# One program in place of two in a gated delta-rule layer: setup joined to the heads, gate logits summed by shifted weights, x's norm on ScalarE, the last norms cut in pieces

## The chip, the cores and the metric

The kernel runs on one core of one Trainium2 chip. The metric is the device time of one execution in microseconds (us); lower is better. The engines of the core are named as in the profile: PE (TensorE; PEld is its weight load), DVE (VectorE), ACT (ScalarE), POOL (GpSimd) and SP (SyncE), which here only issues DMAs. Each engine runs its own instructions in order, and waits on semaphores for the others.

## What is computed

The input x is 8 sequences of 512 tokens with 256 features. `_layernorm` has no weights.

```python
x = x + _layernorm(_L0_attn_ref(_layernorm(x), Wqkv, Wz, Wb, Wa, conv_w, A_log, dt_bias, norm_w, Wout))
x = x + _layernorm(_L0_ffn_ref(_layernorm(x), W1, b1, W2, b2, W3, b3))

# _L0_attn_ref: 16 heads, q, k and v of 128 features each
qkv = silu(causal_conv_4_taps(x @ Wqkv));  z = x @ Wz
beta = sigmoid(x @ Wb)                                  # one logit for a head and a token
g = -exp(A_log) * softplus(x @ Wa + dt_bias)            # another one
q, k = l2norm(q) * 128**-0.5, l2norm(k)
for each token:                                         # M is 128 x 128 for a head
    M = M * exp(g);  M = M + k (v - k M) * beta;  o = q M
out = (o * rsqrt(mean(o*o) + 1e-6) * norm_w * silu(z)) @ Wout
# _L0_ffn_ref: 256 -> 512 -> 512 -> 256, with relu after the first two layers
```

## The kernel before, in words

**Two programs.** `gated_delta_mlp` runs `normalise_and_gate` (the setup) and then `delta_heads`. Between them all semaphores of the first are cleared and all engines meet (L69).

**Setup.** Eight sequences b go through a loop. DVE: `statistics(b + 1)` (L186 to L192), `normalise(b)` (L197: four operations of 128x256), `low_parts(b - 1)` (L204). POOL takes the root of the variance (L173, a `pow` on 128x4). PE transposes the normed x (L293) and multiplies it by the gate weights (L304: six matmuls of 512 columns). ACT copies the transposed x as its rounded high part (L266) and the 32x512 logits (L271). Each product in this kernel that needs full precision is three matmuls: high by high, high by low, low by high. SP stores the logits and the two parts of x^T in DRAM (L148, L152). Then the logits of all sequences are read back from DRAM with one (head, sequence) pair on each of the 128 partitions (L156, L157), and DVE and ACT make of them beta, the decays and their cumulated products (L228 to L258), a chain of 128x512 operations in which each waits for the one before. The decays go to DRAM as rows (L159, L160).

**Heads.** `delta_heads` loads its weights and constants, splits the first head's weights into high and low (`split`, POOL, L603 and L605) and runs 128 pairs (16 heads by 8 sequences) in a software pipeline written out by hand: in iteration a of `range(PAIRS + LAST_STAGE)` each engine does the projections and the convolution of pair a (`project` L1254, `convolve` L790 and L966, `activate` L802), the block inverse of pairs a-1 and a-2, the state recurrence of pair a-3 (`solve` L1361, `state` L1062, `from_state_k` L1368) and the output of pair a-4 (`gated` L1096, `out_project` L1402, `take_sum` L872, `add` L680). The order on each engine is the order of these calls. `decays(a)` (DVE, L977) needs a row of decays loaded from DRAM.

**Drain.** Iterations a = 128 to 131 have no projection any more. Their `fill` calls put in the start of the feed-forward part, sequence b = a - 128: DVE `fill(0)` is `attn_statistics(b)`, `fill(1)` is `add_input(b)` (norm of the attention's sum L1121, addition of x L1136, statistics of the second norm L1109 to L1116), `fill(2)` is `normed_input(b)` (L1121 into `xn`). POOL `root` (L713) takes the two roots; POOL's `split_second` (L690, L692) and `split_third` (L700, L702) split the weights of layers 2 and 3 in quarters: a cast and a subtraction for each. In DVE's order `state(2, a - 3)` and `residual(a - 2)` stand behind `fill(1)`, and the next iteration stands behind `fill(2)`.

**Feed-forward loop.** For b = 1 to 7, PE does `second_layer(b, 0..2)`, `turn_input(b + 1)` (L1419, eight transposes of `xn`), `second_layer(b, 3)`, `first_layer(b + 1, 0..3)`, `third_layer(b)` (all L1425). All turned tiles and all hidden tiles take turns in two PSUM banks, g0 and g1. ACT does `turned_high` (L882) and `hidden` (L897, L900), POOL `hidden_low` (L708) and `root`, and DVE in its iteration b: `result(b)` (L1160 and statistics of four chunks), `finish(b)` (norm L1121 and addition L1168), `turned_low(b + 2)` (L1149), `normed_input(b + 3)`, `attn_statistics(b + 4)`, `add_input(b + 4)`.

## Time and profile before

| | us |
|---|---|
| median of the 3 timed runs (2787.2 to 2790.44) | 2787.56 |
| the profiled execution, its own time | 2786.65 |
| its span, first to last instruction | 2784.90 |
| setup: start to the first convolution step on DVE | 107.02 |
| gate math: its first to its last operation | 65.58 to 87.76 |
| iterations a = 128 to 131 and the first third layer, about | 2485 to 2592 |
| feed-forward loop and end | 2597 to 2785 |

The page gives the busy time of each engine over the whole span; the windows view gives it by stage; the timeline shows the order on each engine, with the idle time before an instruction and what ended it in square brackets. The granted clock of PE is a share: 1.00 is 2.4 GHz, 0.50 is 1.2 GHz, and a value between is a mean of stretches at either.

### The profile page before, as it was taken

How to read it: one execution, taken by the hardware profiler on the slowest of the kernel's cores; microseconds unless marked ns; L12 is line 12 of the kernel's file. 1: busy time of each engine (PE TensorE's matmuls, PEld its weight loads, DVE VectorE, ACT ScalarE, POOL GpSimd, SP SyncE). 2: the span in 40 equal slices, each digit the busy share in tenths (PEclk: the TensorE clock that was granted, in tenths of full speed). 3: DMA queues.
4: the chain of work that ended last, by engine and by line, in shares of the span. 5: the costliest groups of instructions: out<-in, count | busy, mean ns of one | idle time of the engine just before them, and what ended most of it. 6: DMA issues, size and time to landing. Idle time of an engine off the chain costs nothing.

```text
span 2784.9 us, 70958 instructions
## 1 busy us (share of the span) xinstructions
PE 2636.6 (95%) x23924; PEld 2308.0 (83%) x23924; DVE 2305.1 (83%) x4996; ACT 2189.9 (79%) x7350; POOL 2023.3 (73%) x1802
## 2 busy tenths in 40 slices
PE   3399999999999999999999999999999999997898
PEld 2288888888888888888888888888888888885776
DVE  5588888888888888888888888888888888885683
ACT  2388888888888888888888888888888888873343
POOL 2267777877777787777777877777787777775553
PEclk9799999999999999999999999999999999997999
DMA  5322222222222222222222222222222223210110
GB/s 197 112 80 102 92 88 83 102 92 72 99 94 91 81 100 94 79 90 101 89 82 92 102 75 88 100 92 79 94 100 80 91 92 125 71 58 23 31 39 23
DMA packets 81011, 241.94 MB, mean 87 GB/s; under 512 B 8720, under 2 KB 23952, under 8 KB 64272
## 3 DMA queue, kind: packets, MB, share of 16 engines
q1 hardware_dynamic: 80656, 237.41, 24.4%
q8 instruction: 198, 3.24, 0.5%
q14 instruction: 157, 1.29, 0.2%
HBM read 223.75 MB, written 13.63 MB: 85 GB/s over the span
## 4 chain that ended last, share of the span: by engine, by line
PE 86%; DVE 4%; issue 2%; POOL 2%; ACT 1%; DMA 0%; SPq 0%; DVEq 0%; POOLq 0%; ACTq 0%
PE pj L1254 25%; PE pj L1402 9%; PE tr L1261 9%; PE g L1301 8%; PE st L1361 5%; PE op L1381 4%; PE op L1382 4%; PE st L1391 4%; PE st L1368 3%; PE bk L1320 2%; PE bk L1331 2%; PE bk L1334 2%; PE g L1425 2%; PE bk L1351 1%; PE g L1320 1%
## 5 line engine op out<-in xcount | busy, mean ns | idle before, releaser
L966 DVE SCALAR_TENSOR_TENSOR conv<-pj,cw,conv 128x511 f32<-128x511 f32 (+2 forms) x1152 | 847.5, 745 | 54.6 <-ACT conv L790 40.6
L1254 PE MATMUL pj<-xt,w_hi 128*128 128x512 f32 x2048 | 684.3, 415 | 17.3 <-ACT y L779 17.3
L644 POOL TENSOR_TENSOR kq<-kq,cum 128x512 f32<-128x512 f32 x256 | 442.0, 1747 | 0.0
L1254 PE MATMUL pj<-xt,w_lo 128*128 128x512 f32 x1024 | 404.0, 395 | 0.0
L1254 PEld LDWEIGHTS pj<-xt,w_hi 128*128 128x128 f32 x2048 | 348.4, 190 | 63.8 <-ACT y L779 17.7
L673 POOL TENSOR_TENSOR inv<-inv,x 128x512 f32<-128x512 f32 x128 | 148.3, 1159 | 340.0 <-ACT inv L849 340.0
L790 ACT ACTIVATE conv<-pj,cw 128x512 f32<-128x512 f32 x384 | 266.4, 694 | 123.3 <-PE pj L1254 113.3
L1043 DVE TENSOR_TENSOR y<-bk,mask 128x256 f16<-128x256 f32 x512 | 216.5, 423 | 163.7 <-PE bk L1320 157.3
L680 POOL TENSOR_TENSOR attn<-attn,part 128x512 f32<-128x512 f32 x256 | 326.6, 1276 | 0.0
L809 ACT ACTIVATE squares_out<-tr 128x128 bf16<-128x128 f32 x1024 | 273.7, 300 | 46.0 <-PE tr L1261 46.0
L1402 PE MATMUL pj<-wo,yt 128*128 128x256 f32 x1024 | 285.5, 401 | 0.8 <-DVE yt L1096 0.8
L841 ACT ACTIVATE x<-bk 128x256 f16<-128x256 f32 x512 | 196.5, 384 | 111.9 <-PE bk L1334 100.9
L611 POOL TENSOR_TENSOR b<-b,f 128x512 f32<-128x512 f32 x128 | 149.4, 1167 | 142.8 <-DVE f L1005 142.8
L1301 PE MATMUL g<-kq 128*128 128x256 f32 x1024 | 242.3, 379 | 0.0
L809 ACT ACTIVATION_READ_ACCUMULATOR squares_out<-tr 128x1 f32 x1024 | 235.2, 231 | 0.0
L1254 PEld LDWEIGHTS pj<-xt,w_lo 128*128 128x128 f32 x1024 | 193.0, 188 | 45.2
L784 ACT ACTIVATE u<-st,f 128x128 f32<-128x128 f32 x512 | 195.7, 382 | 42.9 <-PE st L1361 20.5
L872 ACT ACTIVATE part<-pj,oc 128x256 f32<-128x256 f32 x512 | 215.5, 477 | 16.3 <-POOL oc L667 6.6
L1361 PE MATMUL st<-r,inv 128*128 128x128 f32 x1024 | 216.5, 293 | 3.2 <-DVE r L1078 1.6
L1361 PEld LDWEIGHTS st<-r,inv 128*128 128x128 f32 x1024 | 164.3, 190 | 57.1 <-DVE r L1078 23.9
L1301 PEld LDWEIGHTS g<-kq 128*128 128x128 f32 x1024 | 184.8, 190 | 19.8
L1382 PE MATMUL op<-u,qk 128*128 128x128 f32 x1024 | 198.7, 276 | 0.0
(201 smaller groups left out, 7877.8 us busy)
## 6 DMA issues: line engine op xcount, KB each, us to landing
xt<-xt_scratch SPq DMA_DIRECT2D x128, 1024.0 KB, 4.8
decay<-decay_scratch SPq DMA_DIRECT2D x128, 256.0 KB, 5.3
cum<-cumdecay_scratch SPq DMA_DIRECT2D x128, 256.0 KB, 5.6
w_raw<-in_w_heads SPq DMA_DIRECT2D x16, 512.0 KB, 7.0
xt_scratch<-xt_hi SPq DMA_DIRECT2D x8, 512.0 KB, 2.8
xt_scratch<-xt_lo SPq DMA_DIRECT2D x8, 512.0 KB, 3.8
x_in<-in_x SPq DMA_DIRECT2D x8, 512.0 KB, 4.2
out<-kq SPq DMA_DIRECT2D x16, 256.0 KB, 2.3
```

Of the source, the lines that this page charges most:

```text
L644: last = nc.gpsimd.tensor_tensor(part, part, of(cum, p)[:, :], ALU.mult)
L680: nc.gpsimd.tensor_tensor(rows, rows, part[:, 2 * i:2 * i + 2, :], ALU.add).then_inc(added[i], 1)
L790: nc.scalar.activation(conv[:, i, :], pj[:, i % 2, :], ACT.Copy, scale=cw[:, i, p // NSEQ, TAPS - 1:TAPS]).then_inc(pre[i], 1)
L809: last = nc.scalar.activation(squares_out[:, row, c, :], tr[:, c, :], ACT.Square, accum_out=of(sums, p)[:, row, c:c + 1])
L966: nc.vector.scalar_tensor_tensor(out=conv[:, i, j:SEQ], in0=pj[:, i % 2, 0:SEQ - j], scalar=cw[:, i, p // NSEQ, TAPS - 1 - j:TAPS - j], in ...
L1043: nc.vector.tensor_tensor(y[level][:, :, :].rearrange("p c (g two w) -> p c g two w", two=2, w=w)[:, :, :, 0, :], ps[:, 0:CH * HALF].rearr ...
L1254: last = nc.tensor.matmul(pj[:, i % 2, :], w[:, kt, cols], x_[:, kt, :], start=(n == 0), stop=(n == 3 * KT - 1))
L1261: last = nc.tensor.transpose(tr[:, c, :], src(c), ident[:, :])
L1301: last = nc.tensor.matmul((g0, g1)[c // 2][:, cols], of(kq, p)[:, 0, chunk(c)], of(kq, p)[:, :, chunk(c)], start=True, stop=True)
L1361: nc.tensor.matmul(st[:, 1, :], of(inv, p)[:, c, :], r[:, c, :], start=True, stop=True).then_inc(w_done[c], 1)
L1382: mm = nc.tensor.matmul(op[:, c, :], of(qk, p)[:, c, :], u[:, c, :], start=(c == 0), stop=True)
L1402: last = nc.tensor.matmul(pj[:, i, DM * (c % 2):DM * (c % 2) + DM], yt[:, chunk(c)], of(wo, p // NSEQ)[:, :], start=True, stop=True)
```

## The change

**Start.** `normalise_and_gate` is gone; `delta_heads` does the setup at its head, with no barrier, on its own buffers: x^T of the eight sequences goes through six places that overlie buffers of the heads, and the last two sequences in the loop (order 2..7, 0, 1) stay in `xt[0]` and `xt[1]`, where pairs 0 and 1 find them. x comes in eight loads. The loop is now, on DVE, `statistics_of_x(i + 1)`, `low_x(i)`; on POOL `root_of_x(i)` (the `pow`, then a multiplication that gives the shift), with one `split` of the first head's weights after each of roots 1 to 4; on ACT `normed(i + 1)` (four 128x256 activations with a bias and a scale from memory) and then `high_x(i)`; on PE `turn_x(i + 1)`, `gate_logits(i)`.

**Gates.** The gate weights stand in a zero-padded tile, 8 columns apart. A window of 128 columns that is shifted by the sequence's number puts a head's logit on partition 8 h + b and zeros elsewhere, so that all sequences add up in two PSUM banks (beta's and the decay's): 12 matmuls a sequence. The way through DRAM (L148, L156, L157) is gone. Of the gate math, the `max` moves under an activation, the memset of `tc` to POOL, the last reciprocal behind the scan. `take_beta` and `decays(0)` move to the end of DVE's iteration 0. ACT's constants (`y`, `ident16`) come before its last gate exponential, and the `memset` of `attn` goes behind the setup.

**Semaphores.** Groups of semaphores for the chunks (`tap`, `w_done`, `u_ready`, `km_done`, `mu_done`, `m_ready`, `w_copied`) become one each that is counted on, in the order in which they were signalled before.

**Drain and feed-forward loop.** The norms on DVE come in ten pieces of two chunks each, spread over the iteration, with the last two (`xn`) at the head of the next. The high parts of the weights of layers 2 and 3 are cast by ACT (`high_weights`, two of 128x512 in each of iterations 128 to 130, ahead of `take_sum(0)`), and POOL subtracts in two operations of 128x512. From b = 2 on the turned x goes to the banks `tr` and `bk`, and `turn_input(b + 1)` stands ahead of `second_layer(b, 2)`; `turned_high` moves likewise. `result` and `finish` work by halves.

```diff
-            statistics(0)
-            for b in range(NSEQ):
-                if b + 1 < NSEQ:
-                    statistics(b + 1)
-                normalise(b)
-                if b:
-                    low_parts(b - 1)
-            low_parts(NSEQ - 1)
+            statistics_of_x(0)
+            for i in range(NSEQ):
+                if i + 1 < NSEQ:
+                    statistics_of_x(i + 1)
+                low_x(i)
+            gate_decays()
...
+            def normed(i):
+                act.wait_ge(rstd_done, 2 * i + 2)
+                for c in range(CH):
+                    last = nc.scalar.activation(of(xin, i)[:, c, :], of(xin, i)[:, c, :], ACT.Identity,
+                                                bias=shift[:, i % 3, c:c + 1], scale=rs[:, i % 3, c:c + 1])
+                last.then_inc(x_normed, 1)
+
+            def high_x(i):
+                if i >= 6:
+                    act.wait_ge(xt_out[i - 6], 2 * DMA)
+                for kt in range(KT):
+                    act.wait_ge(turned_x, KT * i + kt + 1)
+                    nc.scalar.activation(xt_at[i][0][:, kt, :], turn_bank[(KT * i + kt) % 4], ACT.Copy).then_inc(hi_done, 1)
+
+            normed(0)
+            for i in range(NSEQ):
+                if i + 1 < NSEQ:
+                    normed(i + 1)
+                high_x(i)
...
+            def root_of_x(i):
+
+                pool.wait_ge(s_var_done, i + 1)
+                nc.gpsimd.tensor_tensor(rs[:, i % 3, :], ve[:, i % 3, :], halves[:, 1, :], ALU.pow).then_inc(rstd_done, 1)
+                pool.wait_ge(rstd_done, 2 * i + 1)
+                nc.gpsimd.tensor_tensor(shift[:, i % 3, :], shift[:, i % 3, :], rs[:, i % 3, :], ALU.mult).then_inc(rstd_done, 1)
+
+            pad_gate_weights()
+            for i in range(NSEQ):
+                root_of_x(i)
+                if 1 <= i < 5:
+                    split(i - 1, 0)
...
+            def gate_logits(i):
+
+                window = slice(GAP - FIRST[i], GAP - FIRST[i] + P)
+                hi, lo = xt_at[i]
+                for kt in range(KT):
+                    pe.wait_ge(hi_done, KT * i + kt + 1)
+                    for gate_ in range(2):
+                        for w in (wg_hi, wg_lo):
+                            nc.tensor.matmul(logit_bank[gate_], w[kt][:, gate_, window], hi[:, kt, :],
+                                             start=(i == 0 and kt == 0 and w is wg_hi), stop=False)
...
             for a in range(PAIRS + LAST_STAGE):
                 convolve(V, 3, a - 1)
+                fill(8, a)
                 mask_level(3, a - 2)
                 inverse_norm(a - 1)
+                fill(9, a)
                 decay_b(a - 1)
...
                 mask_level(5, a - 2)
-                decays(a)
+                if a:
+                    decays(a)
+                fill(0, a)
                 mask_level(1, a - 1)
...
                 convolve(Q, 1, a)
-                fill(0, a)
+                fill(1, a)
                 convolve(Q, 2, a)
                 mask_level(2, a - 1)
                 convolve(Q, 3, a)
+                fill(2, a)
                 convolve(K, 1, a)
-                fill(1, a)
+                fill(3, a)
                 convolve(K, 2, a)
+                fill(4, a)
                 state(2, a - 3)
                 convolve(K, 3, a)
+                fill(5, a)
                 residual(a - 2)
                 rhs(3, a - 3)
                 convolve(V, 1, a)
-                fill(2, a)
+                fill(6, a)
                 convolve(V, 2, a)
+                fill(7, a)
                 norms(a)
+                if a == 0:
+                    take_beta()
+                    decays(a)
...
+    def turned_tile(b, kt):
+
+        return sums_of(place["turn", b, kt]) if b < 2 else (flat(tr), bk[:, :])[kt]
...
             for b in range(1, NSEQ):
-                for n in range(HT - 1):
+                for n in range(HT):
+                    if n == HT - 2 and b + 1 < NSEQ:
+                        turn_input(b + 1)
                     second_layer(b, n)
-                if b + 1 < NSEQ:
-                    turn_input(b + 1)
-                second_layer(b, HT - 1)
```

## Rows read from the trace of the kernel before

**Rows 1.** The page, part 1: busy time of each engine.
```profile
PE 2636.6 (95%) x23924; PEld 2308.0 (83%) x23924; DVE 2305.1 (83%) x4996; ACT 2189.9 (79%) x7350; POOL 2023.3 (73%) x1802
```
**Rows 2.** Windows, 400 us of pairs: stretch, length, busy us, granted clock, DMA.
```profile
600.00:1000.00 400.00, 399.85 (x3802) 352.47 (x3801) 349.30 (x749) 346.16 (x1197) 315.16 (x280) 1.00 0.25 91
```
**Rows 3.** Timeline, one pass of the setup loop: start, length, instruction, idle before.
```profile
35.49 1.39 DVE L186 BATCH_NORM_STATS2 stats<-xin 128x6 f32<-128x256 f32 x4
...
37.28 1.37 DVE L197 TENSOR_SCALAR xin<-xin,mv,rstd 128x256 f32<-128x256 f32 x4
...
37.45 1.24 POOL L173 TENSOR_TENSOR rstd<-rstd,minus_half_s 128x4 f32<-128x4 f32 x1 [3.03 <-DVE rstd L192]
37.83 1.05 ACT L266 ACTIVATE xt_hi<-s_ps 128x512 fp32r<-128x512 f32 x2
...
38.58 1.28 DVE L204 TENSOR_TENSOR xt_lo<-s_ps,xt_hi 128x512 fp32r<-128x512 f32 x2
...
39.77 1.39 DVE L186 BATCH_NORM_STATS2 stats<-xin 128x6 f32<-128x256 f32 x4
```
**Rows 4.** Lines view, whole span: forms that stand nearest to the new operations.
```profile
L872 ACT ACTIVATE part<-pj,oc 128x256 f32<-128x256 f32 x512 | 215.5, 477 | 16.3 <-POOL oc L667 6.6 <-issue 1.6 <-PE pj L1402 0.9
...
L841 ACT ACTIVATE x<-bk 128x256 f16<-128x256 f32 x512 | 196.5, 384 | 111.9 <-PE bk L1334 100.9
...
L680 POOL TENSOR_TENSOR attn<-attn,part 128x512 f32<-128x512 f32 x256 | 326.6, 1276 | 0.0
...
L702 POOL TENSOR_TENSOR w_lo<-w_raw,w_hi 128x256 fp32r<-128x256 f32 x4 | 2.9, 733 | 0.3
```
**Rows 5.** Timeline of ACT in the drain: four activations of `take_sum` in a row.
```profile
2550.98 1.57 ACT L872 ACTIVATE part<-pj,oc 128x256 f32<-128x256 f32 x4 [2.38 <-POOL oc L667]
```
**Rows 6.** DMA view, first 18 us: KB each, us from issue to landing.
```profile
xin<-in_x SPq DMA_DIRECT2D x1, 512.0 KB, 4.1
```
**Rows 7.** Timeline of the gate math.
```profile
65.58 0.49 DVE L228 TENSOR_SCALAR al<-al,dtb 128x512 f32<-128x512 f32 x1 [8.89 <-DMA al<-logits_scratch]
...
79.59 0.43 DVE L243 TENSOR_SCALAR al<-al 128x512 f32<-128x512 f32 x1
...
80.97 0.72 ACT L279 ACTIVATE tb<-td,rate 128x512 f32<-128x512 f32 x1 [13.05 <-DVE rate L246]
81.43 3.35 DVE L249 RECIPROCAL bl<-bl 128x512 f32<-128x512 f32 x1
...
85.81 1.22 DVE L256 TENSOR_TENSOR_SCAN td<-tb,tc 128x512 f32<-128x512 f32 x1
```
**Rows 8.** Timeline, the first convolution steps on DVE.
```profile
107.02 4.54 DVE L966 SCALAR_TENSOR_TENSOR conv<-pj,cw,conv 128x511 f32<-128x511 f32 x6 [3.77 <-ACT conv L790]
```
**Rows 9.** Timeline of PE in the drain: its long waits.
```profile
2508.20 0.80 PE L1368 MATMUL st<-m,kq 128*128 128x128 f32 x2 [5.02 <-DVE m L1062]
...
2536.03 0.80 PE L1368 MATMUL st<-m,kq 128*128 128x128 f32 x2 [5.16 <-DVE m L1062]
...
2567.11 0.56 PE L1368 MATMUL st<-m,kq 128*128 128x128 f32 x2 [4.34 <-DVE m L1062]
...
2596.83 0.76 PE L1425 MATMUL g<-h_hi,xt 128*128 128x512 f32 x1 [4.70 <-POOL last_h L708]
```
**Rows 10.** Timeline of DVE in iteration 128.
```profile
2504.61 1.23 DVE L1136 TENSOR_TENSOR attn<-attn,x_in 128x1024 f32<-128x1024 f32 x1
...
2512.30 2.96 DVE L1121 TENSOR_SCALAR xn<-attn,mmv,rs 128x256 f32<-128x256 f32 x4 [2.85 <-POOL rs L713]
```
**Rows 11.** PE's waits from 2600 us to the end: us in total, times, longest.
```profile
PE g L1425 <- DVE x_lo L1149: 8.0, 6, 1.4
```
**Rows 12.** Timeline, one pass of the feed-forward loop.
```profile
2634.51 1.28 DVE L1149 TENSOR_TENSOR x_lo<-g,x_hi 128x512 fp32r<-128x512 f32 x2
2635.25 0.50 PE L1425 MATMUL g<-h_hi,xt 128*128 128x512 f32 x1 [1.39 <-DVE x_lo L1149]
```
**Rows 13.** Windows, one such pass: PE, PEld, DVE, ACT, POOL, granted clock, DMA.
```profile
2630.40:2657.10 26.70, 24.97 (x129) 21.00 (x129) 20.59 (x46) 11.54 (x19) 14.01 (x12) 0.94 0.13 40
```

More of the change, by code:

```diff
@@ L961, in _, with take_beta @@
+            def take_beta():
+                dve.wait_ge(beta_turned, 1)
+                then(nc.vector.tensor_copy(beta[:, :, :], logit_bank[1].rearrange("p (c n) -> p c n", c=CH)))
+            statistics_of_x(0)
+            for i in range(NSEQ):
+                if i + 1 < NSEQ:
+                    statistics_of_x(i + 1)
+                low_x(i)
+            gate_decays()
             dve.wait_ge(consts_in, 7 * DMA)
```

694 lines of the change are left out of this document (340 added, 354 removed).

## The prediction, made before the changed kernel ran

> **What bounds the kernel now.** I read the busy times first: PE 2636.6 of 2784.9 us [rows 1]. The windows then say where that is a bound: between 600 and 1000 us PE is busy for 399.85 of 400 us at the full clock [rows 2]. The 128 pairs are PE's, and nothing there can gain unless PE's own work shrinks; the change leaves that work alone. What is left are the two ends, where PE waits. The setup holds the first convolution step on DVE back until 107.02 us [rows 8]. In the drain PE waits three times for a state from DVE, 5.02, 5.16 and 4.34 us, and once 4.70 us for POOL [rows 9]. In the feed-forward loop it waits six times for `x_lo`, 8.0 us in all [rows 11], and a pass of 26.70 us has PE busy for 24.97 us at a mean clock of 0.94 [rows 13].
>
> **Setup loop: no gain, rather a loss.** Before, a pass takes 39.77 - 35.49 = 4.28 us [rows 3], paced by DVE, which holds statistics, `normalise` (1.37) and `low_parts`; roots and ACT work go on beside it. In the new order each step waits for the one before, across engines: DVE does statistics(i+1) only after low(i-1); POOL's root(i+1) needs them; ACT has `normed(i+1)` ahead of `high_x(i)`; low(i) needs `high_x(i)`. One pass is therefore the sum of the chain. Statistics to the start of the root: 37.45 - 35.49 = 1.96, and 0.08 for the added shift operation. Root 1.24. Second POOL operation, 128x4, plus two handovers: the trace has no such multiplication. Its bounds are 0.1 and 1.24 (the `pow` itself); a POOL operation with two inputs takes 733 ns on 256 columns and 1276 on 512 [rows 4], so the fixed part is near 0.2; I take 0.3 and 0.2 for the handovers. `normed`: four activations with one pointer take 1.57 us [rows 5]; a pointer costs 477 - 384 = 93 ns [rows 4] and there are two, so 1.57 + 4 x 0.09 = 1.95. From the start of the high part to the end of the low part: 39.77 - 37.83 = 1.94 [rows 3]. Sum 1.96 + 0.08 + 1.24 + 0.5 + 1.95 + 1.94 = 7.7 us a pass, against 4.28. The bounds of the unknown step give 7.4 and 8.6. The splits (a cast of some 0.4 and 0.73) fit beside it on POOL, the 12 gate matmuls and 8 transposes too (some 4 us of PE in a pass); the exports to DRAM (1 MB a pass) wait on nothing that DVE needs.
>
> The Trainium skill, page "ScalarE: Activation LUTs", section "What ACT_TABLE_LOAD costs", gives about 93 ns for each pointer operand of an activation; the trace agrees (477 against 384). Its section "Rules for kernel authors" speaks against this part of the change: additions and multiplications belong on VectorE. By the trace the same four operations take 1.37 on DVE [rows 3] and 1.95 on ACT, so by that rule the eight passes would be some 4.6 us shorter had they stayed in the chain on DVE; a loop with both engines at work at once would pay for that, but this one doesn't let them.
>
> The loop starts earlier, though. x of the first sequence lands 4.1 us after its issue [rows 6], so at about 4.9; the gate weights' padding on POOL stands ahead of the first root (two strided copies, two casts, two subtractions, some 3 us after the weights land): I put the first root at 9.2, the end of low(0) at 16.8. Six passes of 7.7 bring low(6) to 63.0; low(7) and the last gate matmuls need 2.1 more: the gate math starts at 65.1. Before it started at 65.58 [rows 7]. The longer passes eat all of what the early start and the missing trip through DRAM give.
>
> **Gate math to the first pair: -21.6.** From the first operation to the exponential that gives the decays it was 80.97 - 65.58 = 15.4 us [rows 7]. The `max` (0.43 + 0.04) goes under ACT, one multiplication merges (0.4), the rate's sign is done earlier (0.2); a read from PSUM adds 0.1: 14.4. Then 0.8 for the exponential, 0.4 for the starts, 1.22 for the scan, 3.35 for the reciprocal behind it and handovers: DVE is free for the first convolution step 20.3 us after the start, at 85.4. ACT's two first convolution activations and PE's first two projections are done by then. Before: 107.02 [rows 8]. So -21.6: the barrier, the second round of loads and the splits, which stood between 87.8 and 103, now lie under the setup. Back come `take_beta` and `decays(0)` at the end of iteration 0, 0.7 + 1.2 on DVE and a short wait for PE's transposes, all ahead of the third convolution step of v: +2.5; and some 0.3 for PE at half clock, which it had before too. **Start: -19** (-11 to -26: the unknown POOL step, six to eight passes of up to 0.9, and 4 us for where the first root falls). SP's queue holds the exports, then the decays; the first decay row is wanted only at the end of iteration 0.
>
> **The pairs: 0.** Same instructions, same number of waits; a count on one semaphore is reached in the order in which the single ones were. PE hides it; bounds are in the rivals.
>
> **Drain: -13.** In iterations 128 to 130 the state that PE waits for stands behind the whole of `add_input`. Behind the new order it has half of the addition (0.6, of 1.23 [rows 10]) and the second statistics with their variance (1.39 + 0.4 + 0.1, [rows 3]) less ahead of it: 2.6 us, of waits of 4.3 to 5.2 [rows 9], so it is all felt. After that, `xn` waited 2.85 us for its root and then held `mask_level` for 2.96 [rows 10]; now the root is taken under the end of the iteration, and half of `xn` (1.5) stands ahead of `mask_level`. What is late next is the root itself, about 1.1 us at the head of the next iteration. Net I take 1.2. Three iterations: 3 x 3.8 = 11.4. In iteration 131 POOL's queue (split of w3, root, `hidden_low`) is what PE's 4.70 comes from; four casts of 0.4 leave it, 1.6 to 2.0, and the subtractions cost the same (2 x 1.28 for 4 x 0.73 [rows 4]). ACT takes the casts as 2 x 0.6 in each iteration, ahead of `take_sum(0)`; there ACT is waiting for POOL's `oc` anyway (2.38 us in rows 5), so I cost it at nothing, and at 1.2 x 3 where that cover is gone. Bounds: -3 (only the state moves, and the casts are paid) and -19 (all four waits of rows 9).
>
> **Feed-forward loop: -20.** The pass of 26.70 us holds 1.73 of PE idle and, at a clock of 0.94, about 12% or 3.2 us at half clock, which is 1.6 lost [rows 13]: 3.3 us in each of the six passes. Both come from one place: `second_layer(b, 3)` waits for a bank that DVE has not emptied, 1.39 us, and runs slow after it (0.50 for a matmul [rows 12]; the next ones start 0.43 apart instead of 0.23). Turned tiles in `tr` and `bk` take that wait away. What is late next: `first_layer(b+1)` needs both `x_lo`. DVE ends them at 2634.51 + 1.28 = 2635.8 [rows 12]; in the new order PE would come to it after the transposes and four blocks of twelve matmuls instead of three, that is at 2635.25 - 1.39 - 0.3 + 2.7 = 2636.3. A margin of half a microsecond: thin, since DVE's `finish` is no shorter. DVE's own pass is 20.6 busy of 26.7 [rows 13], so a pass of 23.3 holds it. Bounds: -5 (`x_lo` late by 1 to 1.4 and the clock falling behind it) and -21.
>
> **End: -0.7.** Two of four last statistics (half of 1.39) are done before the last half of the result.
>
> **Sum.** 2786.65 (the profiled execution's own time) - 19 - 13 - 20 - 0.7 = 2734. The median of the runs shown is 0.9 above that execution: **2735**.
>
> **The rivals.**
> (1) The forecast, chance 0.62, own range 2720 to 2748.
> (2) The `x_lo` margin isn't there, and the drain's next wait is close behind the one removed: -5 in the loop and -6 in the drain, -19 at the start: 2757. For it: the margin of 0.5 us, and DVE operations that run at 2.96 instead of 1.37 [rows 10, 3] when POOL works beside them. Against: 26.7 us passes have room. Chance 0.20.
> (3) The setup loop isn't a chain in effect (passes stay near 4.3 to 5): the gate math starts at some 43 to 48: 2735 - 20 = 2715. Against: the order of the calls on ACT and DVE leaves no other reading. Chance 0.08.
> (4) The change does not reach the first pair: something in SP's queue (decays out, then in) or POOL's attention memset holds iteration 0 as long as before: start 0, 2754. Chance 0.06.
> (5) Slower: the counted semaphores, with the buffers at other addresses, make each of 128 pairs longer. Place: the pairs, where PE has 0.15 us of slack in 400 [rows 2]; nothing would hide it. 53 us over 128 pairs: from 0.41 us a pair (of about 18.7) the kernel is as slow as before; at 0.5 us it is 2799. For it: only that no slack is left. Against: waits, matmuls and their order on PE are the same. Chance 0.04.
>
> **How the numbers follow.** Predicted is the likeliest, 2735. From 2716 to 2760 I take in (1), (2), (4) and nearly a share of (3), and leave out the far ends of each. This kernel's measurement can tell 0.2%, 5.6 us, from no change: faster 0.94, same 0.02 (a mild form of (5)), slower 0.04.
>
> **What would show it.** Right: the start of the first low parts' passes 7.4 to 8.6 us apart, first gate operation at 62 to 68 us, first convolution step at 82 to 89; no `y`-wait of PE at 103; PE's waits for `m` in the drain 2 to 3 us; no wait of PE for `x_lo`, passes of 23.1 to 23.6 us at clock 1.00. Wrong: passes of 26 us with the wait now at `first_layer`; a pair's period other than before; a PE wait for ACT in the drain behind `high_weights`.

## The result, and the profile after

The changed kernel takes 2741.39 us (median of 4 runs, 2738.59 to 2742.53) against 2788.07 for the kernel before on the same chip (2787.2 to 2790.44): ratio 0.9829, 95% interval 0.9813 to 0.9844. The forecast was 2735, with 2716 to 2760 around it. The profiled executions of the two kernels differ by 44.2 us in their own time (2786.65 and 2742.43). A second set of runs of the changed kernel (e14_control) gave 2743.89, ratio 0.9841 (0.9826 to 0.9857); its trace is called the second trace of the changed kernel below.

The page, part 1, of the changed kernel (to be held against [rows 1]: PE's busy time grew by 3 us, its span fell by 44):

```profile
span 2740.6 us, 71042 instructions
## 1 busy us (share of the span) xinstructions
PE 2639.9 (96%) x23972; PEld 2315.8 (84%) x23972; DVE 2298.7 (84%) x4976; ACT 2199.1 (80%) x7380; POOL 2013.3 (73%) x1799
```

The way to find where 46.7 us went is to read the same mark in both traces. `yt` is the DVE operation that makes a pair's gated output, just before its output projection. `yt` of the first pair (before at 171.88, after at 151.72) closes the start. `yt` of iteration 128 (2493.61 and 2472.26), `yt` of iteration 131 (2575.27 and 2549.76) and the start of `second_layer(1, 0)` (2596.83 and 2569.50) bound the drain. The start of `third_layer(7)` (2768.21 and 2724.70) closes the loop.

| stretch | forecast | first trace | second trace |
|---|---|---|---|
| start, to `yt` of the first pair | -19 | -20.2 | -18.0 |
| pairs, to `yt` of iteration 128 | 0 | -1.2 | -1.2 |
| drain, to `second_layer(1, 0)` | -13 | -6.0 | -7.2 |
| loop, to `third_layer(7)` | -20 | -16.2 | -16.7 |
| end | -0.7 | -0.8 | -2.2 |

The spans differ by 44.3 us where the steps of the forecast add up to 52.7, because the drain gave half of what was forecast and the loop four fifths. The 1.2 us in the pairs are no finding: this stretch takes 2320.5 to 2322.4 us in the fourteen traces of this case, 2321.7 in the kernel before.

The setup loop, timeline of DVE (start, length, engine, line, operation, and in brackets the idle time before it with what ended it), against [rows 3]:

```profile
22.22 1.39 DVE L873 BATCH_NORM_STATS2 mstats<-part 128x6 f32<-128x256 f32 x4
23.65 0.38 DVE L876 BATCH_NORM_AGGREGATE mmv<-mstats 128x2 f32<-128x6 f32 x4
24.07 0.17 DVE L878 TENSOR_SCALAR shift<-mmv 128x4 f32<-128x4 f32 x1
24.14 0.16 DVE L879 TENSOR_SCALAR ve<-mmv 128x4 f32<-128x4 f32 x1
28.30 1.29 DVE L885 TENSOR_TENSOR w_lo<-g,w_hi 128x512 fp32r<-128x512 f32 x2 [3.99 <-ACT w_hi L646]
29.51 1.39 DVE L873 BATCH_NORM_STATS2 mstats<-kq 128x6 f32<-128x256 f32 x4
```

A pass is 29.51 - 22.22 = 7.29 us, and DVE stands idle for 3.99 of it while POOL takes the root and ACT norms: the chain of the forecast. The gate math starts at 63.67, the first convolution step is at 83.69 [rows 8 had 107.02].

PE's waits from 2480 us to the end (total us, times, longest), against [rows 9, 11]:

```profile
PE st L1400 <- DVE m L1031: 7.1, 3, 2.7
PE g L1465 <- POOL last_h L543: 6.8, 1, 6.8
PE g L1459 <- DVE xn L1084: 5.5, 2, 4.2
```

The waits for the state `m` have halved: 2.56, 2.70 and 1.85 us, where 2 to 3 each were forecast. Those for `xn` grew, though, to 1.39 and 4.16 us. The kernel before has two more waits here that [rows 9] leave out, one for `xn` and one for ACT's relu of the hidden tile (the same view of its trace):

```profile
PE g L1419 <- DVE xn L1121: 2.8, 1, 2.8
PE g L1425 <- ACT conv L897: 2.4, 1, 2.4
```

The wait for ACT stands just ahead of the one for POOL. It fell to 0.30, so PE comes to POOL's last low part earlier, and the wait there grew from 4.70 to 6.77. The two together stayed at 7.1, and the stretch that holds them is 1.8 us shorter; the 6.77 is no loss by itself.

The windows of a loop pass (length, busy of PE, PEld, DVE, ACT, POOL, granted clock, DMA share, GB/s), against [rows 13]:

```profile
2596.00:2619.50 23.50, 23.04 (x130) 19.80 (x128) 20.70 (x49) 11.49 (x18) 13.45 (x11) 1.00 0.14 46
2619.50:2643.00 23.50, 23.39 (x131) 20.06 (x130) 20.70 (x48) 11.50 (x18) 13.35 (x11) 1.00 0.15 45
```

PE's gaps are 0.46 and 0.11 us and the clock is 1.00: a pass is now PE's own work.

### The profile page after: what moved, and what is told of

Same layout as the page of the kernel before. It is cut to its first block, busy times and chain, and to the rows that moved or that the text cites. A ratio compares the mean times of both kernels' runs of the same rounds, so it can differ in the third digit from the quotient of the medians.

```text
span 2740.6 us, 71042 instructions
## 1 busy us (share of the span) xinstructions
PE 2639.9 (96%) x23972; PEld 2315.8 (84%) x23972; DVE 2298.7 (84%) x4976; ACT 2199.1 (80%) x7380; POOL 2013.3 (73%) x1799
## 4 chain that ended last, share of the span: by engine, by line
PE 90%; DVE 4%; POOL 2%; issue 2%; ACT 1%; DMA 0%; POOLq 0%; DVEq 0%; SPq 0%
PE pj L1284 26%; PE pj L1437 9%; PE tr L1291 9%; PE g L1331 8%; PE st L1393 5%; PE op L1413 4%; PE op L1414 4%; PE st L1423 4%; PE st L1400 3%; PE g L1465 3%; PE bk L1352 2%; PE bk L1363 2%; PE bk L1366 2%; PE bk L1383 1%; PE g L1352 1%
## 5 line engine op out<-in xcount | busy, mean ns | idle before, releaser
L694 ACT ACTIVATE squares_out<-tr 128x128 bf16<-128x128 f32 x1024 | 273.0, 300 | 46.7 <-PE tr L1291 46.7
L669 ACT ACTIVATE u<-st,f 128x128 f32<-128x128 f32 x512 | 195.5, 382 | 43.0 <-PE st L1393 21.7
```

The source lines that it names most:

```text
L694: last = nc.scalar.activation(squares_out[:, row, c, :], tr[:, c, :], ACT.Square, accum_out=of(sums, p)[:, row, c:c + 1])
```

## The experiments

Each kernel is the changed kernel with the edit shown; of long edits the main lines are shown, with "..." where others stand. Ratios are to the kernel before on the same chip; to be held against 0.9829 and 0.9841 of the changed kernel.

| run | median us | ratio | 95% interval |
|---|---|---|---|
| e1_stats_ahead | 2728.89 | 0.9785 | 0.9770 to 0.9800 |
| e10_loads_first | 2724.14 | 0.9772 | 0.9757 to 0.9786 |
| e8_norm_on_dve | 2748.34 | 0.9851 | 0.9834 to 0.9867 |
| e2_turn_undone | 2764.94 | 0.9917 | 0.9902 to 0.9932 |
| e3_norm_blocks | 2753.36 | 0.9877 | 0.9862 to 0.9892 |
| e4_pool_casts | 2741.29 | 0.9834 | 0.9817 to 0.9852 |
| e13_short_lows | 2740.84 | 0.9831 | 0.9813 to 0.9848 |
| e5_no_lows | 2741.24 | 0.9835 | 0.9821 to 0.9850 |
| e7_hidden_first | 2736.85 | 0.9815 | 0.9800 to 0.9830 |
| e11_pool_order | 2733.63 | 0.9805 | 0.9789 to 0.9822 |
| e12_all | 2712.12 | 0.9730 | 0.9714 to 0.9745 |
| e14_control | 2743.89 | 0.9841 | 0.9826 to 0.9857 |

**Is the setup loop a chain?** e1_stats_ahead:

```diff
             statistics_of_x(0)
+            statistics_of_x(1)
             for i in range(NSEQ):
-                if i + 1 < NSEQ:
-                    statistics_of_x(i + 1)
+                if i + 2 < NSEQ:
+                    statistics_of_x(i + 2)
                 low_x(i)
```

> The changed kernel, with DVE taking the statistics of x two sequences ahead of the low parts instead of one; nothing else moves. If the setup loop is a chain of one step after the other (7.27 us a pass in the changed kernel: low parts 1.2, statistics 2.1, root and shift 1.3, four normed activations 2.0, one high part 0.6), then statistics and root of the next sequence leave it, and a pass is bounded by the engines' own work: DVE 3.4, ACT 3.1, PE about 4.9 at a clock of 0.9. I expect passes of 4.5 to 5.3 us, the gate math to begin at 46 to 52 us instead of 63.7, and 12 to 18 us off the time: 2726 us where the changed kernel has 2741. Rival: something shared holds the passes anyway, the 1.5 MB that each pass moves (3.9 us at the 400 GB/s that the busiest slices show) or PE at half clock; then a pass stays above 6.3 us and the time falls by under 6 us.

Measured: the first convolution step at 69.90 instead of 83.69, and 12 to 16 us off the time, by the two ratios of the changed kernel. One line of order on DVE gives that; the chain is shown. Around the middle, passes are about 3.7 us apart, shorter than expected, and then DVE waits:

```profile
22.39 1.41 DVE L873 BATCH_NORM_STATS2 mstats<-kq 128x6 f32<-128x256 f32 x4
31.15 1.41 DVE L873 BATCH_NORM_STATS2 mstats<-kq 128x6 f32<-128x256 f32 x4 [5.47 <-DMA kq<-in_x]
35.04 1.41 DVE L873 BATCH_NORM_STATS2 mstats<-part 128x6 f32<-128x256 f32 x4 [0.61 <-DMA part<-in_x]
```

The load of x for the seventh sequence lands late: the next limit is a transfer that the chain had hidden. e10_loads_first is e1_stats_ahead with SP's exports moved behind the loads:

```diff
                 if i + 4 < NSEQ:
                     sp.wait_ge(turned_x, KT * (i + 1))
                     load_x(i + 4)
-                export_xt(i)
+                if i >= 2:
+                    export_xt(i - 2)
...
+            export_xt(NSEQ - 2)
+            export_xt(NSEQ - 1)
```

> The changed kernel with the statistics two sequences ahead, as in the first run, and besides with SP's exports of x^T issued two sequences later, so that the loads of x for sequences 4 to 7 of the loop don't queue behind them. In the first run the passes were 3.7 us until DVE waited 5.47 us for a load; the DMA engines were busy for 0.96 and 0.87 of the time there. If it is the order in the queue, the gate math begins 5 to 8 us earlier than in that run (at about 43 us instead of 49.9) and the time is 2722. If the transfers' sum is the bound (12 MB at some 400 GB/s are 30 us, and the places of the first two sequences must be exported before they are used again), only 0 to 2 us are gained: 2727.

Measured: no wait of DVE for a load after the first three; the gate math starts at 43.4, as expected, and the first convolution step is at 63.44. The order in the queue was the reason, not the sum of the transfers, which stayed the same. (Of the 6.1 us by which `yt` of the first pair came ahead of e1_stats_ahead's, 3.6 to 4.8 are in the time, which at 2724 lies between the two theories' 2722 and 2727; the mark decides.) The windows of this kernel from 16 to 45 us show the bound that is left:

```profile
16.00:30.00 14.00, 14.00 (x76) 11.69 (x75) 12.11 (x47) 11.33 (x24) 6.96 (x12) 1.00 0.80 282
30.00:45.00 15.00, 15.00 (x77) 12.51 (x76) 6.86 (x19) 6.20 (x14) 8.08 (x3) 1.00 1.04 410
```

PE is busy in all of the 29 us, at the full clock. In the second window the DMA engines are full as well (1.04), so what less work on PE would gain there isn't shown. `yt` of the first pair is at 132.47, 19 to 21 us earlier than in the two traces of the changed kernel, and by the ratios 16 to 19 us of that are in the time.

**ACT or DVE for x's norm?** e8_norm_on_dve puts the four operations back on DVE, in the same place of the chain:

```diff
-                    last = nc.scalar.activation(of(xin, i)[:, c, :], ..., ACT.Identity, bias=..., scale=...)
+                    last = nc.vector.tensor_scalar(of(xin, i)[:, c, :], ..., ALU.subtract, ALU.mult)
```

> The changed kernel with x's norm in the setup loop on DVE (four operations of 128x256 with two pointers, 1.37 us) instead of ACT (2.07 us), at the same place of the chain; ACT does only the high parts. By the durations alone a pass gains 0.7 us, 5 us in all: 2736. But ACT's queue is also freed: the high part of sequence i no longer stands behind the norm of i + 1, so it is ready when DVE comes to the low part, and a pass is 1.2 (low parts) + 2.1 (statistics) + 1.4 (root and shift with the handover) + 1.4 (norm) = 6.1 us: 8 us off, 2733. If the chain isn't what bounds the loop, no change.

Measured: not faster (2748.34 us). `yt` of the first pair is at 156.13, 2 to 4 us later than in the two traces of the changed kernel. The middle passes did get shorter (23.51 to 30.01, 6.50 us), and the last statistics start 2.9 us earlier (48.48 for 51.33). But the last norm meets POOL's `memset` of `attn`. Timelines of DVE and of POOL in this kernel, and then of ACT and POOL at the same place of the changed kernel:

```profile
51.96 7.93 DVE L914 TENSOR_SCALAR part<-part,mmv,rs 128x256 f32<-128x256 f32 x4 [1.40 <-POOL shift L589]
...
51.86 6.92 POOL L596 MEMSET attn<- 128x8192 f32 x1
```

```profile
54.82 2.07 ACT L637 ACTIVATE part<-part,shift,rs 128x256 f32<-128x256 f32 x4 [4.24 <-POOL shift L589]
...
54.72 6.94 POOL L596 MEMSET attn<- 128x8192 f32 x1
```

POOL's operation started 0.10 us earlier, and DVE's four operations, 1.38 us when alone, took 7.93: they stood until it had ended. Beside POOL's short split operations (0.40 and 0.72) the same four took 1.90. So a norm on DVE pays for what POOL is doing. The Trainium skill says this on its page "SBUF — State Buffer", section "Who interferes with whom": VectorE in a two-port mode (which `tensor_scalar` can enter) and GpSimd take one shared pair of ports as an exclusive lock for a whole instruction. The trace agrees (7.93 for 1.38). ACT's norm does not pay: it takes 2.07 us in the middle passes and 2.07 beside the `memset`. The rule of the Trainium skill that the forecast weighed ("ScalarE: Activation LUTs", section "Rules for kernel authors") would have kept the norm on DVE, for 4.6 us by the forecast; here one collision outweighs it. A kernel with the norm on DVE and the `memset` later was not run, so which would be faster then stays open.

**The drain: which part gave what?** The drain's marks, in us: `yt` of iteration 128 to `yt` of 131, from there to `second_layer(1, 0)`, and the four `xn` operations after iterations 128, 129 and 130.

| kernel | yt to yt | to second layer | sum | xn x4 |
|---|---|---|---|---|
| before | 81.66 | 21.56 | 103.22 | 2.96, 4.23, 3.19 |
| changed | 77.50 | 19.74 | 97.24 | 4.69, 5.10, 3.24 |
| changed, second trace | 76.19 | 19.82 | 96.01 | 4.69, 5.10, 3.23 |
| e3_norm_blocks | 85.40 | 19.72 | 105.12 | 4.95, 4.16, 2.95 |
| e4_pool_casts | 74.07 | 21.88 | 95.95 | 2.70, 4.23, 3.23 |
| e13_short_lows | 75.22 | 20.46 | 95.68 | 3.29, 4.56, 4.60 |
| e5_no_lows | 75.73 | 20.52 | 96.25 | 2.95, 4.14, 4.19 |

e3_norm_blocks (in `fill` of DVE):

```diff
-                b = a - PAIRS if n < 8 else a - PAIRS - 1
-                if 0 <= b < (4 if n < 8 else 3):
-                    norm_piece(n, b)
+                b = a - PAIRS
+                pieces = {1: (0, 1), 3: (2, 3, 4, 5, 6, 7), 6: (8, 9)}.get(n, ())
+                for k in pieces:
+                    if 0 <= b < (4 if k < 8 else 3):
+                        norm_piece(k, b)
```

> The changed kernel with the drain's norms on DVE back in three blocks at the places of before (statistics, then norm with addition and second statistics, then the norm into xn inside the same iteration); setup, loop, banks and ACT's casts stay as changed. If the pieces are what the drain gained from, PE's waits for the state in iterations 128 to 130 go back from 7.1 us in sum to about 14.5, and the time rises by 5 to 8 us: 2748. What speaks for less: in the changed kernel the last two pieces (xn) stand at the head of the next iteration, where PE's transposes wait for them up to 4.2 us, and that wait goes if the pieces go back; then the time rises by only 1 to 3 us, or not at all.

Measured: the waits for the state are back (15.5 us in sum), and the drain is 7.9 to 9.1 us longer, more than the whole drain had gained. The time rose by 10 to 13, beyond the 5 to 8 expected. So the pieces were worth more than the drain's total, and something else in it lost about 2: with blocks in both, the drain is 105.12 against 103.22 before. By its two parts that is 3.7 more up to `yt` of 131 (85.40 for 81.66) and 1.8 less behind it (19.72 for 21.56). What else differs is the casts on ACT and POOL's subtractions of 128x512 in place of quarters. Two kernels look at these. e4_pool_casts undoes them:

```diff
-                for kt in range(KT):
...
-                    pool.wait_ge(highs, KT * n + kt + 1)
-                    nc.gpsimd.tensor_tensor(lo, raw[:, kt, :], hi.bitcast(F32), ALU.subtract).then_inc(w_split, 2)
...
+                for j in range(HT):
+                    cols = slice(P * j, P * j + P)
...
+                    copied(nc.gpsimd.tensor_copy(hi, raw[:, :, cols]))
+                    nc.gpsimd.tensor_tensor(lo, raw[:, :, cols], hi.bitcast(F32), ALU.subtract).then_inc(w_split, 1)
...
-                elif i == 0 and PAIRS <= a:
-                    high_weights(a - PAIRS)
```

> The changed kernel with one part undone: POOL again casts the weights of layers 2 and 3 itself and subtracts, in quarters of 128x256 (0.40 and 0.73 us each, eight operations an iteration), and ACT has no high_weights; the pieces of the norms stay. Putting the norms back into blocks cost 7.9 us in the drain, more than the whole drain had gained (4.2 us up to yt of iteration 131), so something else in the drain must have lost 3.7. Theory: what lost is POOL's work in operations of 128x512 (1.28 us) in place of 128x256, since each of DVE's normalisations waits for one of POOL's to end; with the short ones back the four xn norms take 3.0, 4.2 and 3.2 us instead of 4.69, 5.10 and 3.24, and yt of iteration 131 comes 2 to 4 us earlier. PE's 6.8 us wait for POOL's last hidden low part grows by up to 1.8, since POOL has the casts again: time 2738 to 2741. Rival: the casts on ACT were right and gave their 1.6 to 2.0 us; then undoing them costs that: 2743.

Measured: the `xn` figures as expected or below (2.70, 4.23, 3.23), `yt` to `yt` 2.1 us shorter than in the second trace and 3.4 shorter than in the first, and 2.1 us given back behind it, where POOL has the casts in its queue again: it finishes the last hidden low part 21.7 us after `yt` of 131 instead of 19.6. PE's wait for it did not grow, as expected, but fell to 5.29, because PE itself comes later: its wait for ACT is back at 2.43. The whole is zero within the scatter: the casts on ACT took 2 us off POOL's queue, as forecast, and as much was lost ahead of `yt` of 131. This edit undoes ACT's casts and POOL's long operations at once, so it doesn't say which of the two cost that. e13_short_lows changes only the length of POOL's operation:

```diff
-                    nc.gpsimd.tensor_tensor(lo, raw[:, kt, :], hi.bitcast(F32), ALU.subtract).then_inc(w_split, 2)
+                    for half_ in range(2):
+                        cols = slice(HID // 2 * half_, HID // 2 * (half_ + 1))
+                        nc.gpsimd.tensor_tensor(lo[:, cols], raw[:, kt, cols], hi.bitcast(F32)[:, cols],
+                                                ALU.subtract).then_inc(w_split, 1)
```

> The changed kernel with the subtractions for the weights' low parts in four operations of 128x256 in each iteration instead of two of 128x512; the casts stay on ACT. If the length of the one POOL operation that DVE has to wait for is what makes the xn norms slow, the four norms of iteration 129 take 3.0 to 3.8 us instead of 4.69 (each waits for 0.73 instead of 1.28), those of 130 under 4.8 instead of 5.10. If it is the share of POOL's busy time, they stay the same. Time: within 2 us of the changed kernel either way.

POOL is busy for 2.97 us with it instead of 2.59, so for longer, and yet `xn` falls from 4.69 to 3.29 and from 5.10 to 4.56. Both are as expected; it is the length of the operation that DVE waits for, not POOL's share of busy time. Of the drain, `yt` to `yt`, it gives 1.0 to 2.3 us (75.22 for 76.19 and 77.50), less than e4_pool_casts. After iteration 130 `xn` rose, though, from 3.24 to 4.60: the norm there fell beside three other operations of 128x512 (POOL, 2544.29 to 2548.14). The lines, DVE and POOL of the changed kernel, then of this one:

```profile
2488.36 2.62 DVE L1084 TENSOR_SCALAR xn<-attn,mmv,rs 128x256 f32<-128x256 f32 x2 [1.13 <-POOL rs L548]
...
2488.30 1.26 POOL L529 TENSOR_TENSOR attn<-attn,part 128x512 f32<-128x512 f32 x1
2489.52 2.59 POOL L538 TENSOR_TENSOR xt<-raw,xt 128x512 fp32r<-128x512 f32 x2
```

```profile
2490.03 2.08 DVE L1087 TENSOR_SCALAR xn<-attn,mmv,rs 128x256 f32<-128x256 f32 x2 [1.13 <-POOL rs L551]
...
2492.36 1.21 DVE L1087 TENSOR_SCALAR xn<-attn,mmv,rs 128x256 f32<-128x256 f32 x2
...
2489.96 1.26 POOL L529 TENSOR_TENSOR attn<-attn,part 128x512 f32<-128x512 f32 x1
2491.19 2.97 POOL L540 TENSOR_TENSOR xt<-raw,xt 128x256 fp32r<-128x256 f32 x4
```

Two norms of 0.35 us each take 2.62, which is two times POOL's 1.3: one DVE operation goes through between two of POOL's.

e5_no_lows leaves POOL's subtraction out for all but 8 columns:

```diff
-                    nc.gpsimd.tensor_tensor(lo, raw[:, kt, :], hi.bitcast(F32), ALU.subtract).then_inc(w_split, 2)
+                    nc.gpsimd.tensor_tensor(lo[:, 0:8], raw[:, kt, 0:8], hi.bitcast(F32)[:, 0:8], ALU.subtract).then_inc(w_split, 2)
```

> The changed kernel in which POOL's six subtractions for the low parts of the weights of layers 2 and 3 work on 8 columns instead of 512 (this leaves work out: the low parts are not filled). Theory: a DVE normalisation of 128x256 can't run while POOL works on a 128x512 operation, and has to take its turn between two of POOL's; that is why the xn pieces take 4.69, 5.10 and 3.24 us for four instead of 1.37. Then the four at 2488 come down to under 2.5 us and those at 2516 to 2 to 4.3 (another low part and the addition into attn are still beside them), PE's 4.16 us wait for xn falls by 1 to 2.5 us, and the time by 1 to 4 us: 2739. Rival: DVE's slow norms come from their own operands or from ACT beside them; then the durations stay within 10%.

Measured: `xn` 2.95 (expected under 2.5), 4.14 (in the range), PE's waits for `xn` 3.7 us in sum instead of 5.5, and nothing in the time. The collision is real, but removing it moves PE's wait rather than ending it: the other operations of POOL and the root for iteration 131 (DVE waited 6.43 us for it, 5.38 in the changed kernel) come next.

**What does PE wait for at the end of the drain?** e7_hidden_first, in POOL's `fill(1)` of iteration 131:

```diff
                     elif i == 1:
                         root(0, b)
+                        if b == 3:
+                            hidden_low(2, 2)
+                            hidden_low(2, 3)
...
```

> The changed kernel with one reordering on POOL in iteration 131: the last two low parts of the hidden layer (those that PE's second layer of sequence 1 waits for, 6.77 us in the changed kernel) stand ahead of the addition into attn and of the second root, which itself waits 4.84 us for DVE. The high parts that they need are ready at 2557.4 and 2559.0, the low parts are finished at 2569.4. If POOL's order is what PE waits for, they are finished near 2561.3, PE's wait goes below 0.5 us, and the time falls by 5 to 7 us: 2735. Rival: the next wait is close behind (x_lo of sequence 2, or result of sequence 0 on DVE, which stands behind the norm of sequence 3), and the time falls by under 2 us.

Measured: the wait of 6.77 is gone, and PE has a new one a little later:

```profile
2579.99 0.47 PE L1468 MATMUL g<-x_hi,w_hi 128*128 128x512 f32 x1 [2.88 <-DVE x_lo L1126]
```

From `yt` of iteration 131 to the first `x_lo` of the loop it is 26.15 us, against 32.37 and 31.86. Most of it stays: from `yt` of 131 to `third_layer(7)` it is 168.89, against 174.94 and 174.49, so 5.6 to 6.1 us less. The wait of 2.88 costs less than it looks, since the first 12 us of this second layer run at a granted clock of 1.00 here and of 0.81 in the changed kernel, whose PE had just waited 6.77. In the time it is 4 to 7 us, by the two ratios. So POOL's order was what PE waited for, as the first theory had it, with a small part of the rival's next wait behind it. e11_pool_order adds to that the root of the attention norm ahead of the second hidden low part and the weights' low parts ahead of the inverse:

```diff
                     if i == 0 and b:
                         hidden_low(b - 1, 0)
-                        hidden_low(b - 1, 1)
                     elif i == 1:
                         root(0, b)
+                        if b:
+                            hidden_low(b - 1, 1)
...
-                        if b < 3:
-                            low_weights(b)
...
+                if PAIRS <= a < PAIRS + 3:
+                    low_weights(a - PAIRS)
                 inverse(a - 2)
```

> The changed kernel with three changes of POOL's order in the drain: the last two hidden low parts of iteration 131 first (measured alone: 4.5 us, with a wait of 2.9 us for x_lo behind it), the root of the attention norm ahead of the second hidden low part, which waits for ACT (DVE waited 2.79, 3.94 and 5.38 us for that root), and the weights' low parts in POOL's idle time ahead of the inverse (3.6 to 5.4 us) instead of beside DVE's norm into xn. Expected: the xn norms take under 2.6 us for four, PE's waits for the state and for xn fall from 12.6 us in sum to about 7, and the time falls to 2729 to 2733. Rival: these waits overlap, since PE's state recurrence goes through all of them, and only the 4.5 us remain: 2737.

Measured: 2733.6, just above the 2729 to 2733 expected, but not by the way expected. The four `xn` norms take 3.12, 4.15 and 4.19, and from `yt` of 128 to `yt` of 131 it is 76.81, no less than before the edit: the earlier norm of `attn` now meets a hidden low part, an addition and the weights' low parts, which this edit put there (5.19 and 3.32 us for four instead of 2.46), and PE's waits for the state are 8.1 us, not less than 7.1; with those for `xn` 10.6 in sum, where about 7 was expected. All of the gain is behind `yt` of 131: 24.29 us to the first `x_lo` instead of 26.15 in e7_hidden_first, since the root that DVE waited 5.38 us for comes in 1.12.

**Are the turned tiles' banks what the loop gained from?** e2_turn_undone puts the turned x back into `g0` and `g1` (place, waits and signals as before) and its transposes ahead of the last block:

```diff
...
-        return sums_of(place["turn", b, kt]) if b < 2 else (flat(tr), bk[:, :])[kt]
+        return sums_of(place["turn", b, kt])
...
-                    if n == HT - 2 and b + 1 < NSEQ:
+                    if n == HT - 1 and b + 1 < NSEQ:
                         turn_input(b + 1)
...
```

> The changed kernel with one part undone: the turned x goes back into the two shared banks g0 and g1, and its transposes stand ahead of the last block of the second layer instead of the one before. If the loop's gain comes from that, PE's wait for the low part comes back (about 1.4 us a pass, with a stretch at half clock behind it), passes are 26.0 to 26.7 us instead of 23.5, and the time rises by 14 to 18 us: 2757. If the loop gained from the halves of result and finish or from the shorter drain instead, the time moves by less than 4 us.

Measured: 21 to 25 us slower, more than expected and more than the loop had gained. PE's waits, in all and the longest:

```profile
PE g L1460 <- DVE x_lo L1124: 12.7, 6, 2.5
```

That is 2.1 us each, where the kernel before had 8.0 in six [rows 11]. The `x_lo` of successive passes are 27.87, 27.66, 27.65, 27.49 and 26.23 apart, mean 27.4; before they were 25.14, 26.67, 26.67, 25.14 and 26.57, mean 26.0; in the changed kernel 23.46, 23.31, 23.22, 23.15 and 22.97, mean 23.2. So the banks, with the transposes one block earlier, are worth 4.2 us a pass; the edit undoes both and doesn't part them. Of the remaining 1.4 over the kernel before, `finish` by halves takes 1.1. `finish` in this kernel's timeline of DVE, to be held against the 2634.51 - 2630.90 = 3.61 us that it took before:

```profile
2635.86 1.72 DVE L1085 TENSOR_SCALAR kq<-kq,mmv,rs 128x256 f32<-128x256 f32 x2 [1.12 <-POOL rs L552]
2637.62 0.69 DVE L1144 TENSOR_TENSOR kq<-kq,attn 128x512 f32<-128x512 f32 x1
2638.23 0.73 DVE L1085 TENSOR_SCALAR kq<-kq,mmv,rs 128x256 f32<-128x256 f32 x2
2638.99 1.68 DVE L1144 TENSOR_TENSOR kq<-kq,attn 128x512 f32<-128x512 f32 x1
2640.60 1.28 DVE L1124 TENSOR_TENSOR x_lo<-g,x_hi 128x512 fp32r<-128x512 f32 x2
```

It takes 4.74: the second addition, with both inputs in SBUF, takes 1.68 instead of 0.69, again beside a POOL operation (a hidden low part, 2638.87 to 2640.13). In the changed kernel `finish` takes 3.73 to 3.85 in the same passes and its second addition 0.69: POOL's low part comes later there, so the loss doesn't arise.

**All improvements together.** e12_all is e10_loads_first with the edits of e11_pool_order.

> Both kernels' setup and drain improved by what the runs before showed: statistics two sequences ahead, loads of x ahead of the exports, and POOL's order in the drain. The two parts lie at opposite ends of the program, and PE is busy throughout between them, so they should add: 2741 - 17 - 7 = 2717. If the setup's gain is partly a shift into a wait of the first pairs (the exports are still running then), 2720.

Measured: 2712.12 us (2711.78 to 2714.15) beside 2743.89 for the unchanged changed kernel in the same rounds, so 31.8 off where 24 were expected, and 2712 for 2717. By the marks, 22.1 us come up to `yt` of the first pair (131.77 for 153.88) and 9.2 between `yt` of 131 and the first `x_lo` (22.64 for 31.86). The spans of the two traces differ by 29.5, since between these stretches the new trace is 2.0 longer, about what single traces scatter by. The two parts add up: alone they gave 16 to 19 and 7 to 10 us by the ratios. This version beats both kernels: 2.7% under the kernel before, 1.2% under the changed one.

**How much do marks move by themselves?** e14_control is the changed kernel again.

> The changed kernel itself, unchanged, on the same chip and in the same rounds as the three others. By all theories 2741 within 2 us. Its trace shows also how much the marks of the drain (yt of iterations 128 to 131, the start of the second layer of sequence 1) move from one execution to another with the same program: I expect under 1 us.

Measured: the time 2.5 above the first set, the ratios within each other's intervals. The marks moved by more than the 1 us expected: `yt` of the first pair is 2.2 us later, `yt` to `yt` in the drain 1.3 shorter. 1.5 of the 2.2 have a place: in this execution gate matmuls of the last two sequences ran at 0.63 us each for a while (0.39 in the first trace). The granted clock from 58.1 to 61.1 us is 0.50, the lower level, and 1.00 in the first trace, though PE was busy for 4.00 of the 7.40 us before 57.4 in both. DVE waited for these matmuls:

```profile
65.20 0.75 DVE L894 TENSOR_SCALAR k_tok<-op,dtb 128x512 f32<-128x512 f32 x1 [5.24 <-PE op L1242]
```

In the first trace it waited 3.72. Differences of 1 to 2 us between single traces, or in time, as those of e5_no_lows and e13_short_lows, are thus no findings; the durations of `xn` in the drain, which repeat to 0.01 us in the two traces, are.

## Why the prediction was right, and where it was not

**The setup loop** came as worked out: 7.27 to 7.29 us a pass for 7.7 (just under the 7.4 to 8.6 given as the sign), gate math at 63.67 for 65.1. The 0.4 too many lies in POOL's two operations with their handovers, 1.32 us for 1.74 (24.39 to 25.71). The chain was shown by breaking it (e1_stats_ahead). That the gate math came within 1.4 us is in part luck: the first low part ended 1.8 earlier than forecast and six passes gave 2.5 more, but from the seventh low part to the first gate operation it was 5.0 us where 2.1 were put down (58.70 to 63.67), since DVE waits 3.72 us for the last gate matmuls. The forecast's aside, that the norm on ACT pays in a loop with both engines at work at once, fits e1_stats_ahead: its passes take 3.7 us, where DVE's own 3.2 and 1.3 for the norm would make 4.5 (an estimate; no run has it). What the forecast did not see is that the norm on DVE would have met POOL: its estimate of 4.6 us in favour of DVE would have held for the middle passes of e8_norm_on_dve (0.8 us in those beside a split, 1.3 in the others) and was more than lost in the one pass beside the `memset` (7.93 - 1.38 = 6.5).

**Gate math to the first pair**: 83.69 for 85.4, and in the second trace 85.22. The sum of durations held. Behind it `take_beta`, `decays(0)` and their waits gave back 3.2 and 3.8 us for the 2.5 forecast, by `yt` of the first pair. Start: -20.2 and -18.0 for -19.

**The pairs**: PE is busy for 399.86 of 400 us between 600 and 1000, as it was [rows 2]; rival 5 had no place in the trace.

**The drain** was mis-sized: -6.0 and -7.2 for -13. Of its three terms the state's waits were right (3 x 2.6 = 7.8 forecast; 14.5 to 7.1, so 7.4, measured). The second, 3 x 1.2 for `xn`, is the step that failed: the forecast took the four `xn` operations at 1.5 us for a half, out of the 2.96 of [rows 10], and put only the root's delay against it; they took 4.69 and 5.10, and with `xn` at the head of the next iteration PE's transposes waited 1.39 and 4.16, where the kernel before has one such wait of 2.84. The pieces gave 7.9 to 9.1 us with the casts on ACT (e3_norm_blocks), 7.3 with the casts on POOL (95.95 for 103.22): about the state's part, and little of the 3.6 for `xn`. The rows had the warning, since the same four operations take 1.37 in [rows 3] and 2.96 in [rows 10]; the forecast named that in a rival and didn't price it. The third, -1.6 to -2.0 for the casts, arrived behind `yt` of 131 and was lost ahead of it (e4_pool_casts). The forecast costed ACT's casts at nothing, and PE's waits for ACT there did not grow (1.7 us for `u` in both traces); what it did not cost was POOL's operations growing from 128x256 to 128x512. How much of the loss is the one and how much the other was not parted: shortening POOL's operations alone (e13_short_lows) brought 1.0 to 2.3 us of it, with the third `xn` longer.

**The loop** was -16.2 and -16.7 for -20. The mechanism was right, down to the margin for `x_lo`: the windows show clock 1.00, and PE waited 0.7 us in all for `x_lo`, in two passes (the longer 0.46), where none was forecast. Only the size was off: 3.3 us a pass was read from one pass of 26.70, and two of the five distances were 25.14. The mean of all, 26.0, less 23.2 is 2.8, and six of these are 16.8.

**The rivals.** The drain half of rival 2 is what happened (-6, "DVE operations that run at 2.96 instead of 1.37 when POOL works beside them"), its loop half did not. Rival 3 (no chain) is refuted by the trace of the changed kernel, but the state that it describes was reached by one line of order: the gate math starts at 43.4 in e10_loads_first, where the rival had 43 to 48, and the time was 2724 where it had 2715, because the drain and the loop had given less. Of the rest, SP's queue is what came next there, though ahead of the gates and not behind them as rival 4 had it.

**Open.** Why the granted clock fell to 0.50 for 3 us of the setup in the second trace and not in the first, with the same work before it, was not found; nothing was tried on it. Two runs are missing that would part causes: the casts on POOL with long subtractions, and x's norm on DVE with the `memset` later.

## What to carry to other kernels

When work is moved between engines, price not only the engine that it leaves and the one that it goes to, but the length of the single operations that then stand on POOL beside DVE's norms, casts and additions: make POOL's operations short there (it shortened `xn` here, though no time was gained by it), or put the norm on ACT, which took its 2.07 us beside POOL too. Where a loop's steps alternate between engines, count how far ahead the first step of the next item is issued: one item more turned 7.3 us a pass into 3.7 here. And read a loop's pass from the mean of all its passes, not from one.

## What the runs showed of the hardware

- A DVE `tensor_scalar` of 128x256 in SBUF, 0.35 us alone, waits for the end of a running POOL operation: 7.93 us for four beside a `memset` of 6.92, 2.62 for two and 5.10 for four beside operations of 128x512 (1.26 to 1.32), 1.90 for four beside a split of 0.40 and 0.72. POOL's own operations kept their durations within 0.1 us beside these norms.
- ACT's norm of the same form (an activation with a bias and a scale from memory) takes 2.07 us for four beside a POOL `memset` of 6.94, as it does alone.
- A DVE addition of 128x512 with both inputs in SBUF suffers as well (1.68 for 0.69), and POOL's operation with it (two subtractions of 128x512 took 3.03 beside such additions of 1.63 and 1.49 in e11_pool_order, 2.59 otherwise). `x_lo`, with one input in PSUM, took 0.68 to 0.69 in every pass of every kernel, beside POOL's low part too (2605.59 in the changed kernel, POOL from 2605.42).
- In the loop POOL's four hidden low parts hold DVE's norm of `attn` for 5.50 us instead of 1.4; it costs nothing there, since PE is the bound.
